# A graph kernel's attention: the value sum of a pair of row tiles in one go, and another order on ScalarE in odd units

## The reference

```python
q = (x @ wq + bq).reshape(N, H, Dh) * Dh ** (-0.5)
k = (x @ wk + bk).reshape(N, H, Dh)
v = (x @ wv + bv).reshape(N, H, Dh)
scores = jnp.einsum('ehd,ehd->eh', q[src], k[dst])
smax = jax.ops.segment_max(scores, src, num_segments=N)
ex = jnp.exp(scores - smax[src])
denom = jax.ops.segment_sum(ex, src, num_segments=N)
attn = ex / denom[src]
out = jax.ops.segment_sum(attn[:, :, None] * v[dst], src, num_segments=N)
return out.reshape(N, D) @ wo + bo
```

## Time and profile before

| what | value |
|---|---|
| median of 3 runs | 1890.31 us (1885.86 to 1890.96) |
| the profiled execution, its own time | 1887.15 us |
| its span, first to last instruction | 1885.4 us |
| TensorE matmul busy | 1826.2 us, 97% |
| TensorE weight load busy | 1521.3 us, 81% |
| VectorE busy | 1097.7 us, 58% |
| ScalarE busy | 754.7 us, 40% |
| GpSimd busy | 327.5 us, 17% |
| mean granted TensorE clock | 0.998 of full speed |

### The profile page before, as it was taken

How to read it: one execution, slowest core, us unless ns; L and a number is a source line. 1 busy time by engine, 2 the same in 40 slices (tenths; PEclk the granted TensorE clock), 3 DMA queues, 4 the chain that set the end, 5 groups by cost and what they waited for, 6 DMA issues and landing times.

```text
span 1885.4 us, 31958 instructions
## 1 busy us (share of the span) xinstructions
PE 1826.2 (97%) x11066; PEld 1521.3 (81%) x11067; DVE 1097.7 (58%) x2302; ACT 754.7 (40%) x1071; POOL 327.5 (17%) x393
## 2 busy tenths in 40 slices
PE   6899999999999999989999999899999999999998
PEld 6887554687888888878888888788888887888887
DVE  6888546634555667345555773355547834555476
ACT  4553221024565431235654412255543212556532
POOL 0000721300000434000003440000016400000163
PEclk9999999999999999999999999999999999999999
DMA  3002200121000110211001011101010112000011
GB/s 120 0 0 98 95 28 34 44 78 56 29 29 1 39 51 23 78 44 38 33 1 39 23 51 54 67 15 44 14 39 23 51 37 83 15 29 29 23 66 66
DMA packets 38731, 79.64 MB, mean 42 GB/s; under 512 B 10856, under 2 KB 10856, under 8 KB 38592
## 3 DMA queue, kind: packets, MB, share of 16 engines
q1 hardware_dynamic: 38592, 77.82, 12.4%
HBM read 66.14 MB, written 11.67 MB: 41 GB/s over the span
## 4 chain that ended last, share of the span: by engine, by line
PE 63%; issue 32%; DVE 1%; ACT 1%; DVEq 1%; POOL 1%; DMA 1%; ACTq 0%; SPq 0%; POOLq 0%
PE ps L1278 39%; PE ps L1303 5%; PE ps L1210 4%; PE ps L1336 4%; PE ps L1268 4%; PE ps L1329 2%; PE ps L1237 2%; PE ps L1342 2%; PE ps L1387 2%; DMA x<-in_x_dram 1%; DVE hot L850 0%; POOL film L527 0%; DVEq L845 0%; PE ps L1391 0%; POOL kh L573 0%
## 5 line engine op out<-in xcount | busy, mean ns | idle before, releaser
L1303 PE MATMUL ps<-pT,v 128*128 128x256 f32 (+1 forms) x1600 | 370.2, 379 | 4.1 <-ACT pT L764 4.1
L703 ACT ACTIVATE s<-masked_s,small 128x1280 f32 (+1 forms) x156 | 213.3, 1367 | 338.2 <-DVE small L983 338.2
L1278 PE MATMUL ps<-yT,w 128*128 128x512 f32 (+1 forms) x1728 | 330.1, 352 | 0.0
L1303 PEld LDWEIGHTS ps<-pT,v 128*128 128x128 f32 x1600 | 292.2, 190 | 42.3 <-ACT pT L764 8.4
L1278 PE MATMUL ps<-kh,q_parts 128*128 128x512 f32 (+3 forms) x1440 | 317.4, 365 | 4.8 <-DVE v L1065 3.4
L1278 PEld LDWEIGHTS ps<-yT,w 128*128 128x128 f32 x1728 | 280.6, 189 | 45.0
L1278 PEld LDWEIGHTS ps<-kh,q_parts 128*128 128x128 f32 (+1 forms) x1440 | 248.5, 189 | 51.7 <-issue 4.8
L1278 PE MATMUL ps<-w,kh 128*128 128x512 f32 (+1 forms) x960 | 235.4, 396 | 2.4 <-POOL kh L573 2.4
L764 ACT COPY pT<-ps 128x1408 f32<-128x1408 f32 (+1 forms) x160 | 206.7, 1292 | 3.9 <-PE ps L1391 3.9
L1278 PEld LDWEIGHTS ps<-w,kh 128*128 128x128 f32 (+1 forms) x960 | 174.3, 186 | 41.3 <-POOL kh L573 2.8
L980 DVE CUSTOM_DVE_ANT_0 masked_s<-ps,mask 128x1280 f32<-128x1280 f32 x96 | 143.2, 1491 | 91.3 <-PE ps L1278 91.3
(11 more groups left out here) (167 smaller groups left out, 1983.9 us busy)
## 6 DMA issues: line engine op xcount, KB each, us to landing
mask<-mask_dram SPq DMA_DIRECT2D x24, 640.0 KB, 4.0
w_raw<-in_L_gnn_m_w_dram SPq DMA_DIRECT2D x8, 1024.0 KB, 5.3
mask_y<-mask_dram SPq DMA_DIRECT2D x12, 640.0 KB, 4.6
mask_dram<-mask_out SPq DMA_DIRECT2D x10, 640.0 KB, 2.9
w_l<-in_L_gnn_W_dram SPq DMA_DIRECT2D x2, 2048.0 KB, 10.1
w_raw<-in_L_gnn_wq_dram SPq DMA_DIRECT2D x4, 1024.0 KB, 5.4
w_raw<-in_L_gnn_wk_dram SPq DMA_DIRECT2D x4, 1024.0 KB, 5.4
w_raw<-in_L_gnn_wv_dram SPq DMA_DIRECT2D x4, 1024.0 KB, 6.2
```

The lines of the kernel that those rows point to most:

```text
L703: nc.scalar.activation(to, masked_of(u), ACT.Exp, bias=small[0:R, u % 2, 1:2], accum_out=small[0:R, u % 2, 2:3]).then_inc(exp_done, 1)
L1278: mine = mm(to, left(a), right(b), start=first and n == 0, stop=final and n == 2)
L1303: mine = mm(ps[:, 6 + gh % 2, 0:wd], v[:, t, h * P:(h + 1) * P], pT[:, gh % 2, t, 0:wd], start=(t == 0), stop=(t == NT - 1))
```

## The change

Two edits of order in `attention`, on TensorE and on ScalarE. No instruction is added or removed, and no buffer or semaphore changes.

```diff
@@ ScalarE, attention
-                    if u + 1 < U:
+                    if u + 1 < U and k == 0:
                         exp(u + 1, i)
...
                     nc.scalar.copy(pT[:, gh % 2, :, k * P:k * P + R], turn[:, :, 0:R]).then_inc(pT_out, 1)
+                    if u + 1 < U and k == 1:
+                        exp(u + 1, i)
@@ TensorE, attention
                     if u + 1 < U:
                         scores(u + 1, i)
-                    if u >= 2:
-                        weigh(u // 2 - 1, k, i)
+                    if u >= 2 and k == 0:
+                        for part in range(2):
+                            weigh(u // 2 - 1, part, i)
```

## The result

The changed kernel takes 1963.92 us (median of 4 runs, 1956.32 to 1966.69) against 1890.47 us before (median of 4 runs, 1885.86 to 1890.96): a ratio of 1.0386, with a 95% interval of 1.0361 to 1.0411. It is slower by 73 us. The forecast was 1959 us.

The account below looks back on a forecast made before the run. The attention was taken as bound by TensorE. A sum of 17.60 us per block, 70.4 for four, gave 1957.6 us from the profiled execution or 1960.7 from the median; forecast 1959, 8 in 10 for 1942 to 1971.

Parts of the forecast that it names:

- The new wait: Odd units: with only the turn between two sets of scores, TensorE waits for VectorE's mask step, 0.89 us per pair.
- The loop itself: Scores' end to mask step 0.22, mask step 1.49, its end to the next scores 0.12: 1.83 us through one bank set.
- The stall removed: Even units: the value sum no longer waits for ScalarE's copy behind the exp; 0.21 us per pair gone.
- The late exp hidden: Odd units' exp starts later, 0.2 us on ScalarE, nothing on TensorE, since the 4.3 us value sum covers it.
- rival 3: A second wait in the even unit because the exp is later: 38 us more, some 1997 us; 4%.
- The length of a pair: Steady attention pair: scores 1.99, value sum 4.32, turn 0.94, scores 1.74, loop 1.83: 10.82 us against 9.88.
- 17.6 us per block: Attention block: all pairs' changes summed, +13.16 of it from pairs 2 to 15; 70.4 us for four blocks.
- rival 2: Attention: the clock falls to 1.2 GHz for a tenth of TensorE's work, 56 us more, 2015 us; 3%.
- that tail: Block's end, last pair: the half value sum no longer covers the last copies; 8.73 us becomes 10.09, +1.36.
- The rule of the Trainium skill: Frequent short idles while cycling through PSUM banks make TensorE's clock switch levels; cost would exceed the sum.
- Rival 1: Odd units: the mask step's loop is covered, so the change wins; pair 9.68 us, in all 1876 us; 3%.
- unit 0: Block's first unit, no value sum between scores: the wait already shows, 0.84 us without weight load, 0.63 without matmul.

Follow-up runs that it names:

- split_8_2: Changed kernel with the value sum split, 8 key tiles in the even unit and 2 in the odd one; 1892.9 us.
- longer_loop: Changed kernel plus one VectorE maximum ahead of the mask step of even units, which runs in the odd unit; 2009.3 us.
- longer_covered: Changed kernel plus the same kind of VectorE maximum ahead of the mask step of odd units, beside the value sum; 1966.0 us.
- merged_in_odd: Kernel before with the whole value sum in the odd unit, exp ahead of copy in all units as before; 1953.4 us.
- the three splits: Changed kernel with 7, 8 or 9 of 10 value sum tiles in the even unit, the rest in the odd one; 1876.8, 1892.9 and 1927.8 us.
- merge_only: Kernel before with only TensorE's edit: whole value sum in the even unit, ScalarE's order as before; 2055.3 us.
- swap_only: Kernel before with only ScalarE's edit: copy ahead of exp in odd units, value sum in halves as before; 1908.5 us.
- last_pair_halves: Changed kernel, but in the last pair of a block's units the value sum is done in halves as before; 1951.7 us.
- shifted: Kernel before with each half of the value sum a unit later, head outputs moved along, ScalarE's order as before; 1872.9 us.
- split_9_1: Changed kernel with the value sum split, 9 key tiles in the even unit and 1 in the odd one; 1927.8 us.
- split_7_3: Changed kernel with the value sum split, 7 key tiles in the even unit and 3 in the odd one; 1876.8 us.

## Why the prediction was right

*The new wait.* The prediction's wait was "1.83 - 0.94 = **0.89 us per pair**": measured 60.3 / 76 = 0.79 us without a matmul on average. The loop itself was 1.71 in the chain (1689.66 to 1691.37) instead of 1.83: 0.16 to the mask step instead of 0.22, 0.06 behind it instead of 0.12. Both short pieces of mine came out 0.06 too long, the scores in the odd unit 0.02 too short (1.76 for 1.74). These are modelled ends: in the chain of `split_8_2` the first piece is 0.23 again (1611.59 to 1611.82). From weight load to weight load the odd unit is 3.80 us in all kernels whose odd unit is set by the loop alone, be there no, one or two tiles in it. `longer_loop`, `longer_covered`, `merged_in_odd` and the three splits show that it is this loop, and not the copy, the turn or the amount of VectorE's work.

*The stall removed.* As forecast: the value sum waits for no copy. `merge_only` shows that the new order on ScalarE is needed for that.

*The late exp hidden.* As forecast in the merged kernel, and rival 3 did not occur. The mask step behind the late exp ends at 1684.61, and the scores that need it start their weight load at 1687.61, 3.0 us later, straight behind the turn:

```profile
1683.13 1.48 DVE L982 CUSTOM_DVE_ANT_0 masked_s<-ps,mask_w 128x1280 f32<-128x1280 f32 x1
...
1687.61 1.82 PEld L1280 LDWEIGHTS ps<-kh,q_parts 128*128 128x128 f32 x9
```

`swap_only` shows what happens when the cover is only a half sum: the pair is 0.17 us longer than before, and a wait of 0.2 us shows.

*The length of a pair.* 10.82 forecast, 10.77 measured. The value sum of 4.32 us in one piece and the 2.0 us of scores after a wait came out to 0.03 us.

*The attention in all.* 17.6 us per block were forecast. From the end of GpSimd's film step (L527) at the start of the attention to the product behind the last value sum, the four blocks are 18.1, 19.9, 20.4 and 18.1 us longer. Without the 8.6 us of clock these are 67.9 us, 17.0 per block.

*The clock.* I gave a fall of the clock (rival 2) 3% and a price of 56 us. In the attention it did not come: a gap of 0.8 us in each pair left the granted clock at 0.99 to 1.00. But at the block's end, of which I had only said that the half sum "covered the last copies", a gap of 1.7 us came up, and the clock was down behind it in all four blocks. I had costed that tail at +1.36 us per block and nothing for the clock; the tail itself came out at 1.4, and the clock was about 2.1 more, 8.6 us in all. `last_pair_halves` gives nearly all of both back. `swap_only` shows that a half sum there is no sure cover, as my sentence had it: with the copy behind the late exp its gap was 1.5 to 1.6 us all the same. The rule of the Trainium skill ("TensorE: Matmul & The Clock Gate", "A second HAM failure mode: psum-queue depth-cycling") thus has no support in the steady part of this kernel, and the falls at its end came with a gap twice as long, and only 11 transposes between it and the next.

*The rest.* 3.1 us of the difference between the two profiled executions lie ahead of the first attention (its first film step ends at 438.1 before and 441.2 after), where no instruction was moved. Why is not shown; executions of the kernel before differ by 5 us among themselves.

*What was luck.* The mechanism and its price held, but that the total came within 5 us of 1959 is partly luck: the clock's 8.6 us stood in no term, the attention without it came out 2.5 us under the sum, and four executions of the changed kernel spread over 10 us.

*Rival 1*, that the loop is covered, falls with the 76 waits. Its price was right, though: the pair of 9.68 us that it gave for a covered loop is the one that `shifted` measures.

## What to carry to other kernels

Work between two steps that share a single buffer is cover for whoever empties the buffer; before merging or moving it, add up the loop through the other engine and compare it with what is left in between. The price of the loop often stands in the trace already, at the start or end of a loop where the cover is missing: here unit 0 gave it to 0.1 us. And a stall that comes from a late partner was cured here by taking the work a step later, and not by clumping it.

## What the runs showed of the hardware that I had not expected

A wait that ends before TensorE's matmuls would be idle still costs: in `split_8_2`, scores released just as the turn ended took 1.98 us in the chain instead of 1.74, with no idle time listed for the matmuls.

Whether the granted clock falls at the end of a block's attention went with the gap ahead of the last turn, read from the weight loads of all twelve kernels. With a gap of 1.2 to 1.75 us, followed by 11 transposes and another gap of 0.4 to 0.9 us, the first product of the next stage ran at the lower level in 19 of 32 blocks (4 of 4 in the changed kernel, 4 in `merge_only`, 3 in `split_9_1`, 2 each in `longer_loop`, `longer_covered` and `split_7_3`, 1 each in `split_8_2` and `swap_only`). With a gap of 0.2 to 0.7 us it did in none of 16 (the kernel before, `last_pair_halves`, `merged_in_odd`, `shifted`; the last has no second gap either, the other three have it at 0.7 to 0.9). A fall costs up to 2.8 us. It may also be why the times of the changed kernel spread over 10 us: its fastest run had a mean clock of 0.994, its slowest 0.989; that was not tried. What decides in a single block stays open.
